# An attention kernel with group norm: where VectorE aggregates the next image's statistics and makes its norm, and where ScalarE makes the seed

## The reference

```python
def _gn(v, G=32, eps=1e-05):
    g = v.reshape(B_, G, C_ // G, H_, W_)
    m = jnp.mean(g, axis=(2, 3, 4), keepdims=True)
    s = jnp.var(g, axis=(2, 3, 4), keepdims=True)
    return ((g - m) / jnp.sqrt(s + eps)).reshape(v.shape)

def _L0_conv_ref(x, qkv_w, temp, out_w, out_b):
    xt = x.reshape(b, c, n).transpose(0, 2, 1)
    w = jnp.einsum('bnc,oc->bno', xt, qkv_w).reshape(b, n, HEADS, d).transpose(0, 2, 1, 3)
    norm = jnp.sqrt(jnp.sum(w * w, axis=-2, keepdims=True))
    w_normed = w / jnp.maximum(norm, 1e-12)
    s = jnp.sum(w_normed * w_normed, axis=-1)
    Pi = jax.nn.softmax(s * temp[None, :, :], axis=1)
    Pi_n = Pi / (jnp.sum(Pi, axis=-1, keepdims=True) + 1e-08)
    dots = jnp.einsum('bhn,bhnd->bhd', Pi_n, w * w)[:, :, None, :]
    attn = 1.0 / (1.0 + dots)
    out = -(w * Pi[..., None]) * attn
    out = out.transpose(0, 2, 1, 3).reshape(b, n, c)
    out = jnp.einsum('bnc,oc->bno', out, out_w) + out_b
    return out.transpose(0, 2, 1).reshape(b, c, hh, ww)

x = x + _L0_conv_ref(_gn(x), L0_conv_qkv_w, L0_conv_temp, L0_conv_out_w, L0_conv_out_b)
```

## Time and profile before

| | us |
|---|---|
| median of 3 runs | 894.88 (894.17 to 894.91) |
| profiled execution | 893.38 |
| its span | 891.6 |
| matmuls busy | 859.2 (96%) |
| VectorE busy | 741.2 (83%) |
| ScalarE busy | 524.6 (59%) |
| GpSimd busy | 225.7 (25%) |

### The profile page before, as it was taken

How to read it: one execution, slowest core, us unless ns; L and a number is a source line. 1 busy time by engine, 2 the same in 40 slices (tenths; PEclk the granted TensorE clock), 3 DMA queues, 4 the chain that set the end, 5 groups by cost and what they waited for, 6 DMA issues and landing times.

```text
span 891.6 us, 14234 instructions
## 1 busy us (share of the span) xinstructions
PE 859.2 (96%) x4322; PEld 683.9 (77%) x4322; DVE 741.2 (83%) x1368; ACT 524.6 (59%) x676; POOL 225.7 (25%) x101
## 2 busy tenths in 40 slices
PE   6799999999999999999999999999999999999996
PEld 5477787777787777787777787777778777778785
DVE  7598888889888889888889888889888888888755
ACT  4576555676555667555667555667655667655621
POOL 1331133331133331133332123332123333123300
PEclk9899999999999999999999999999999999999999
DMA  7315655545664444665544665544565544564432
GB/s 274 128 49 192 221 194 178 164 164 185 219 220 154 173 158 178 218 220 159 180 151 176 217 220 163 199 143 168 208 220 190 180 144 169 198 220 151 147 113 104
DMA packets 54852, 158.47 MB, mean 178 GB/s; under 512 B 21426, under 2 KB 25778, under 8 KB 50866
## 3 DMA queue, kind: packets, MB, share of 16 engines
q1 hardware_dynamic: 46048, 155.48, 50.7%
q10 hardware_dynamic: 8786, 2.77, 1.2%
HBM read 105.70 MB, written 52.53 MB: 177 GB/s over the span
## 4 chain that ended last, share of the span: by engine, by line
PE 26%; DMA 25%; ACT 18%; issue 14%; DVE 13%; SPq 3%; ACTq 1%; DVEq 0%
PE acc L485 24%; DMA PIB<-pi 18%; DMA pi<-PIT 6%; ACT WV L393 5%; DVE WV L781 3%; ACT WS L384 3%; ACT XH L412 3%; ACT XN L401 3%; ACT UH L374 3%; SPq L301 2%; PE scores L565 2%; SPq L296 1%; DVE PIT L743 1%; DVE WS L755 1%; ACT log_var L352 1%
## 5 line engine op out<-in xcount | busy, mean ns | idle before, releaser
L334 POOL TENSOR_TENSOR XL<-XN,XH 128x1024 fp32r<-128x1024 f32 x93 | 222.6, 2410 | 602.6 <-ACT XH L412 599.0
L384 ACT ACTIVATE WS<-acc 128x1024 f32<-128x1024 f32 x96 | 98.3, 1024 | 243.0 <-PE acc L485 226.9
L485 PE MATMUL acc<-XH,W1H 128*128 128x512 f32 x576 | 178.9, 392 | 2.9 <-ACT XH L412 2.8
L485 PE MATMUL acc<-UH,W2H 128*128 128x512 f32 x576 | 178.6, 391 | 3.1 <-ACT UH L374 3.1
L485 PE MATMUL acc<-UH,W2L 128*128 128x512 f32 x576 | 178.3, 391 | 0.0
L485 PE MATMUL acc<-XH,W1L 128*128 128x512 f32 x576 | 178.2, 391 | 0.0
L799 DVE SCALAR_TENSOR_TENSOR X<-acc,bias,X 128x1024 f32<-128x1024 f32 x96 | 120.1, 1276 | 60.7 <-PE acc L485 60.6
L374 ACT ACTIVATE UH<-WV 128x1024 fp32r<-128x1024 f32 x96 | 98.1, 1054 | 94.3 <-DVE WV L781 94.0
L485 PE MATMUL acc<-UL,W2H 128*128 128x512 f32 x576 | 150.2, 396 | 0.0
L485 PE MATMUL acc<-XL,W1H 128*128 128x512 f32 x576 | 147.9, 392 | 0.8 <-DVE XL L700 0.8
L755 DVE CUSTOM_DVE_ANT_0 WS<-PIB,WS 128x1024 f32<-128x1024 f32 x96 | 117.0, 1223 | 18.7 <-DMA PIB<-pi 17.1
(11 more groups left out here) (78 smaller groups left out, 434.1 us busy)
## 6 DMA issues: line engine op xcount, KB each, us to landing
PIB<-pi SPq DMA_DIRECT2D x96, 528.0 KB, 6.1
out_y<-X SPq DMA_DIRECT2D x96, 512.0 KB, 7.3
X<-in_x SPq DMA_DIRECT2D x31, 1536.0 KB, 6.3
gathered<-stats_rows ACTq DMA_DIRECT2D x30, 72.0 KB, 6.6
pi<-PIT SPq DMA_DIRECT2D x96, 16.5 KB
X<-in_x SPq DMA_DIRECT2D x3, 512.0 KB, 4.7
WV<-in_L_conv_qkv_w SPq DMA_DIRECT2D x1, 576.0 KB, 6.6
WS<-in_L_conv_out_w SPq DMA_DIRECT2D x1, 576.0 KB, 7.5
```

The lines of the kernel that those rows point to most:

```text
L334: pool.tensor_tensor(XL[:, t, :], XN[:, t, :], XH[:, t, :].bitcast(F32), ALU.subtract).then_inc(xl_done, 1)
L384: act.activation(square_tile(i, t), acc[:, t, :], ACT.Square, accum_out=sumsq[:, t:t + 1]).then_inc(squared, 1)
L485: last = pe.matmul(out[:, h * BANK:(h + 1) * BANK], w[:, k, m * P:(m + 1) * P], r[:, k, h * BANK:(h + 1) * BANK], start=(n == 0 and k == 0 ...
```

## The change

On VectorE, the aggregation of the next image's statistics moves from ahead of the weighing to behind UL 1, directly ahead of the head-sum weights. The norm moves from behind the weighing to behind the head-sum weights, ahead of UL 2. On ScalarE, the two activations of the seed move from behind `u_hi(0)` to behind the square of tile 2, where they stood already for image 0. No instruction is added or taken away.

```diff
@@ step of ScalarE
                 square_w(0)
                 keep_w(0)
                 u_hi(0)
-                if i.follows(1):
-                    group_seeds(i + 1)
                 square_w(1)
                 u_hi(1)
                 u_hi(2)
                 square_w(2)
-                if has(i) and not i.follows(1):
+                if has(i):
                     group_seeds(i + 1)
                 keep_w(1)
                 keep_w(2)
@@ step of VectorE
                 for k in range(4):
                     attention(i - 1, k)
-                group_moments(i + 1)
                 weigh(i - 1, 0)
                 weigh(i - 1, 1)
                 weigh(i - 1, 2)
                 if not has(i) and has(i - 1):
                     finish(i - 2, 2)
-                group_norm(i + 1)
                 u_lo(i - 1, 0)
                 u_lo(i - 1, 1)
+                group_moments(i + 1)
                 head_sum_weights(i)
+                group_norm(i + 1)
                 u_lo(i - 1, 2)
```

## The result

| | us |
|---|---|
| median before (4 runs, 893.68 to 894.91) | 894.52 |
| median after (4 runs, 878.82 to 881.03) | 879.63 |
| ratio, 95% interval | 0.9836 (0.9819 to 0.9853) |
| forecast, and its range | 882.3 (879.0 to 887.0) |
| profiled execution after, its span | 878.82, 877.0 |

The kernel is 14.9 us faster, 2.3 more than the forecast saving of 12.6, and inside the range, 0.6 above its lower end.

What follows compares the result with a forecast made beforehand. A ring through the statistics' transfers (26.55 us an image) was taken as the bound. Gaps closed, 0.6 + 12.6 = 13.2 us, less 0.6 lost at TensorE's switch, save 12.6: 894.88 - 12.6 = 882.3 us, range 879.0 to 887.0.

Steps and rivals of the forecast that it cites:

- The ring of statistics: Statistics write to VectorE's aggregation 10.80 us, from there to the next write 15.75; claimed to set the 26.55 us period.
- Part 1, the aggregation: VectorE's aggregation goes behind UL 1: its 0.87 us wait for the gathered statistics goes, leaving about 5 us of slack.
- Part 2, the norm: VectorE's norm, 1.08 us, goes behind the head-sum weights, which are reached 0.87 + 1.08 = 1.95 us earlier; no cost.
- Part 3, the seed: ScalarE's two small activations, 0.54 us, leave the way to the last square; at most some 0.1 us of wait.
- What is late next, the squares: ScalarE's squares, which inv waits for, become late next; 0.43 us to spare in the loop, so TensorE's gap closes whole.
- The ring through Pi: From softmax through Pi's transfer, dot 2 and VectorE's work back to softmax: 25.68 us, 0.47 to spare under 26.15.
- The switch inside the loop: TensorE's start of the head sums in the loop: 0.11 us lost, at most 0.20; 0.6 us lost in all.
- The rival of weights loaded ahead: TensorE loads head-sum weights early, so the 0.09 us gap goes in the loop too: 879.1 us, chance 0.06.
- Image 1: This image's own gap before the head sums, taken to be 0.71 us, closes by 0.6.

## Why the prediction was right, and where it was not

**What bounded before: right.** The ring of statistics was read off two issues of the write and one aggregation (10.80 + 15.75 = 26.55). That sum is no evidence by itself: from one issue to the next of the same transfer is one period in any loop. The wait at the aggregation is a sign and no proof, as the page's chain leads past it through Pi. The evidence came with the runs. Putting 1.2 us into it cost 1.2 us an image, lengthening it by 0.5 made the kernel slower than before, at the period that was worked out, and the 10.8 us through the transfers stayed the same in all three kernels.

**Part 1, the aggregation: right, and it is the whole gain.** The 0.87 us are gone from ahead of it and the period fell to TensorE's. What the text didn't say, since it added up 1.95 us for the weights, is that the norm's share wasn't needed: with the norm still ahead of the weights, and the aggregation and the seed placed so as to allow it, the period is the same 26.15.

**Part 2, the norm: no cost, as said, and no gain of its own.** UL 2 starts 1.66 after inv (446.64 to 448.30), exactly as worked out, and TensorE's group behind the head sums takes the same 1.49 us as before.

**Part 3, the seed: right.** It follows the square without a wait. It isn't a free move, though: alone it costs 134 us. Left ahead of the square it costs 48 if the aggregation stands behind UL 1, and nothing in the loop if the aggregation stands ahead of UL 0, as the run with the norm ahead shows.

**What is late next, the squares: right.** inv waits 0.16 to 0.29 us for ScalarE in ten images of the loop. The weights end 0.63 to 0.64 us before TensorE starts in most images; the estimate was 0.43 + 0.20.

**The ring through Pi: the mechanism was right, its length was mis-sized.** 25.68 was forecast, 25.97 to 26.02 follows from the runs with added work, so 0.13 us to spare for 0.47. It didn't change the result, because that is still under 26.15 and single late transfers are mostly absorbed. That the period came out at TensorE's own is luck to this extent: 0.2 us more in that ring would by the forecast still have cost nothing, and would have cost time. The dot products' wait, 0.9 us in image 16, is the forecast 1.

**The switch inside the loop: mis-sized.** 0.11 was taken with up to 0.20 as the bound; 0.09 to 0.10 was measured, in the loop as outside. Behind a wait TensorE starts 0.20 after the weights' end inside the loop and 0.10 outside; without a wait the two don't differ, so whatever TensorE does there in the loop no longer costs time. Over images 2 to 31 this made 12.5 us where 12.0 were forecast (12.6 less 0.6), 0.5 of the 2.3 by which the gain was larger. The rival of weights loaded ahead, which the Trainium skill, "TensorE: Matmul & The Clock Gate", Part 2, step 1, would have had close the gap, fell: with weights ready 0.28 to 0.80 us before, 0.09 or 0.10 is lost in all thirty images. The loading of the head-sum weights starts with the head sums themselves, at 421.80, after 0.35 us without a load. The page names conditions for loading ahead; which of them isn't met here no run shows.

**Image 1: the right size for another reason.** Its own gap was to close by 0.6. It grew: the head sums of image 1 wait 0.78 us for the weights, 0.56 before. They come at 55.63 instead of 56.18 all the same, because TensorE gets to them 0.8 us sooner at the head of the run (the head sums of image 0 start at 31.18 instead of 32.35; 1.3 was forecast, and no gain from it). In a second profile of the changed kernel they come at 55.15, so this term moves by half a microsecond by itself.

**The tail: the rest, and luck.** From the head sums of image 31 (853.29 and 840.25) to the end of the span it is 38.3 us before and 36.8 after, 37.7 in the second profile of the changed kernel. These executions differ in the clock that TensorE was granted behind its idle time in that stretch: in the one before and in the second of after it fell, in the first of after it stayed up. The two of the changed kernel, whose code is the same:

```profile
859.00:863.00 4.00, 3.39 (x13) 2.26 (x14) 4.00 (x4) 2.59 (x3) 0.00 (x0) 1.00 0.05 22
```

```profile
859.00:863.00 4.00, 3.91 (x11) 2.92 (x12) 4.00 (x5) 2.12 (x2) 0.00 (x0) 0.59 0.18 74
```

The columns are those of the earlier trace rows; the granted clock is the third number from the end, 1.00 and 0.59. Over all fourteen profiles the tail is 36.5 to 36.8 us in the five where the clock stayed up there, and 37.6 to 38.3 in the nine where it fell, and the kernel before is in both groups (36.8 with 1.2 us of added work). So this microsecond isn't the change's doing in the profiles. Whether it is part of the 14.9 us between the medians can't be told from them. With the switch's 0.5 and this 1.5, the 2.3 us above the forecast are found but for 0.3, which lie between the profiled executions (14.6 apart) and the medians (14.9).

## What to carry to other kernels

When an engine waits and the engine that it waits for is itself idle elsewhere in the same turn, look for a ring: follow one piece of data from its transfer round to the issue of the same transfer one turn later and add up. The sum is the period in any case; look instead for a wait in every turn at the end of the transfer, and for a part that keeps its length when work is added elsewhere in the ring. If it is there, only what is taken out of that ring counts. Moving a wait within an engine's stream can take it off the ring for nothing, if what it feeds is needed later than the new place.

Before calling a move done, work out the length of the next ring with the waits that the new order brings, and put a known amount of idle work into it on the chip: the dose at which the time starts to rise is the slack, which no view of the profile shows directly. Here the smallest dose, 0.6 us, was already more than the slack, and 0.13 is what its rows leave.

Parts of such a change aren't worth something each: here one part alone costs 134 us, two of three cost 13 without the aggregation's move and gain 11 without the norm's, and all three gain 15.

## What the runs showed of the hardware

A tenth of a microsecond is lost where TensorE goes from products with 128 x 128 weights to head sums with weights of 32 columns, though the weights are ready 0.28 to 0.80 us before: 0.09 or 0.10 us in 30 images. On the way back it is 0.13 us.

With 3.3 us of idle time ahead of the head sums in every image, TensorE's granted clock fell behind it to 0.52 (404.80 to 408.20), and TensorE's work of one image took 1.5 us longer.

Adding 1.2 us to the loop brought, once in four images, a delay of 1.2 us in three small writes and the start of the spread that follows them, with little else running on the DMA engines. With 0.6 us one image of thirty had a delay, in the spread and not in the writes; with 1.2 us elsewhere, or in the kernel before, every fourth image showed landings later by 0.6 to 1.0 us. This stays open.
